# One product for q, k and v over two neighbouring PSUM banks, with the order of work rebuilt, in an attention and FFN block

## The chip, the cores and the metric

The kernel runs on one core of a Trainium2 chip. Five engines work side by side, each through its own queue in order: TensorE (PE in the profile, its weight loads PEld), VectorE (DVE), ScalarE (ACT), GpSimd (POOL) and SyncE (SP), which issues transfers. They wait for each other through semaphores. Times are microseconds of the device for one execution; lower is better.

## What is computed

For x of 8 batches x 512 rows x 128 columns:

```python
xn = _layernorm(x)                                  # over the 128 columns
# attention part
q, k, v = split(xn @ w_qkv.T)                       # 16 heads of 8
q = softmax(einsum('bhtd,hcd->bhtc', q, code) * scale) * scale
k = einsum('bhtd,hcd->bhtc', k, code) * scale
k_exp = exp(k - max(k, axis=2))                     # 2 codes a head, max over time
kv = cumsum(k_exp x v, axis=2) / (cumsum(k_exp, axis=2) + 1e-09)
attn = einsum('bhtc,bhtcd->bhtd', q, kv) @ w_out.T
# FFN part, every operand through a blockwise FP4 quantisation (blocks of 16)
h = silu(fp4(xn) @ fp4(w_gate).T) * (fp4(xn) @ fp4(w_up).T)
out = x + attn + fp4(h) @ fp4(w_down).T
```

## The kernel before

A batch of 512 rows is worked on as four tiles of 128 rows (`TILES`), all four side by side in one buffer of 512 columns. The code weights are folded into the q and k weights at the start, so that the product of a tile with `wqk_t` has only 64 columns: 32 for q (`HC`, the difference of the two codes of a head) and 32 for k. The product with `wv_t` has 128.

A batch runs through these stages. ScalarE normalises x into `xn`; TensorE transposes it into the PSUM bank `t_ps`, ScalarE copies it to `xn_t`. TensorE then makes v of the four tiles in `t_ps` (L1458) and, some time later, q and k of the four tiles in `a_ps` (L1591). ScalarE copies v out (`v_sb`, L556) and takes q out (`q_rel`, L674). VectorE reduces the maximum of k over the tiles (`k_max`, L1162), TensorE transposes it (L1692, in `t_ps`), VectorE reduces it to `k_negmax` (L1234), and TensorE adds it to k where k stands in `a_ps` (the shift, L1729). ScalarE writes the exponential of k into `kv` (L786). GpSimd multiplies v into it (L500) and adds up the four tiles (L337, L391, L436). TensorE makes the base of the cumulative sum over the 128 partitions in `a_ps` (L1450); VectorE adds it (L992), makes the denominators (`den`, L1002), which ScalarE inverts through a logarithm and an exponential (`den_log` L607, `a_ps` L609, called dexp below), and after `den_p` and `den_r` makes the normalised q, `q_n` (L1051). GpSimd multiplies it into `o_codes` (L375), TensorE transposes those into `t_ps` (L1660, L1661), ScalarE copies them to `o_t` (L714).

The FFN takes xn through the quantisation: `x_abs`, `x_max`, `x_recip` on VectorE, `x_r` on ScalarE, `yx` on GpSimd, a square on ScalarE into `s_ps`, then `sx` and `qx` on VectorE, `xq` on GpSimd, a transpose into `t_ps` (L1508) and the copy `xq_t` (L587). Four gate and four up products of 352 columns go through the banks `g_ps`, `u_ps0` and `u_ps1`; ScalarE applies silu, VectorE multiplies to `h`, and h is quantised the same way (`h_max`, `h_recip`, `h_r`, `yh`, square, `sh`, `qh`, `hq`), transposed through `h_ps` to `hq_t` and multiplied with the down weights into `o_ps`, where the attention output is added to it (L1410 to L1626). VectorE adds x (`out_sb`, L1187), SyncE stores.

silu and the logarithm and exponential stand in two table sets of ScalarE, so that each batch has two table loads (L629, L784).

The order is written out by hand, or rather as the result of a plan: each engine's block is a loop over steps, and each piece of work stands in it with its own offset (`b = step - 13`), so that one turn of the loop works on several batches at once. The last batch has its own pieces with fixed steps. Waits are written ahead of the piece that needs them; a wait that an earlier one covers is left out. There is one buffer of two for most data (`p = b % 2`) and one bank of PSUM for each of the names above. At the start, short products of constants into `o_ps` stand between TensorE's own work.

## Time and profile before

| | us |
|---|---|
| median of 3 runs | 145.97 |
| lowest, highest | 145.9, 146.12 |
| the profiled execution | 145.66 |
| its span, first to last instruction | 143.9 |

| engine | busy us | share of the span |
|---|---|---|
| PE | 135.2 | 94% |
| DVE | 126.0 | 88% |
| POOL | 120.9 | 84% |
| ACT | 115.2 | 80% |
| PEld | 112.8 | 78% |

The span is read as a head in which weights are prepared and the first batches come in, a middle in which each batch takes the same time (a period), and a tail in which the last batch drains. A busy share over the whole span mixes them, so stretches are looked at apart. Durations of neighbours on an engine overlap by about 0.1 us in the records; the time that an instruction costs its engine is from its start to the start of the next.

### The profile page before, as it was taken

How to read it: one execution, taken by the hardware profiler on the slowest of the kernel's cores; microseconds unless marked ns; L12 is line 12 of the kernel's file. 1: busy time of each engine (PE TensorE's matmuls, PEld its weight loads, DVE VectorE, ACT ScalarE, POOL GpSimd, SP SyncE). 2: the span in 40 equal slices, each digit the busy share in tenths (PEclk: the TensorE clock that was granted, in tenths of full speed). 3: DMA queues.
4: the chain of work that ended last, by engine and by line, in shares of the span. 5: the costliest groups of instructions: out<-in, count | busy, mean ns of one | idle time of the engine just before them, and what ended most of it. 6: DMA issues, size and time to landing. Idle time of an engine off the chain costs nothing.

```text
span 143.9 us, 2675 instructions
## 1 busy us (share of the span) xinstructions
PE 135.2 (94%) x909; PEld 112.8 (78%) x909; DVE 126.0 (88%) x340; ACT 115.2 (80%) x276; POOL 120.9 (84%) x130
## 2 busy tenths in 40 slices
PE   3979999999999999999999999999999998969793
PEld 3979987598869886988698869887988685839692
DVE  0899998999899899989998999899989995999841
ACT  0376788799999989998999899989995797597450
POOL 4567688579999999999889998999599999969920
DMA  4990000000000001000100010001000200010012
GB/s 115 344 343 9 2 0 2 0 0 7 0 0 0 0 5 73 0 0 2 73 5 0 2 73 0 5 0 73 0 0 0 77 0 0 27 48 5 0 73 73
DMA packets 4078, 5.16 MB, mean 36 GB/s; under 512 B 545, under 2 KB 2145, under 8 KB 4065
## 3 DMA queue, kind: packets, MB, share of 16 engines
q1 hardware_dynamic: 3088, 4.49, 8.9%
q10 hardware_dynamic: 976, 0.51, 1.2%
q8 instruction: 7, 0.11, 0.3%
q14 instruction: 7, 0.05, 0.1%
HBM read 2.90 MB, written 2.10 MB: 35 GB/s over the span
## 4 chain that ended last, share of the span: by engine, by line
PE 75%; DVE 11%; ACT 5%; POOL 3%; DMA 2%; issue 1%
PE t_ps L1458 5%; PE a_ps L1591 4%; PE a_ps L1450 3%; PE g_ps L1603 3%; PE u_ps L1570 3%; PE g_ps L1711 3%; PE t_ps L1757 3%; PE u_ps L1574 3%; PE g_ps L1571 3%; PE o_ps L1412 3%; PE u_ps L1654 2%; PE g_ps L1675 2%; PE u_ps L1685 2%; PE o_ps L1626 2%; PE o_ps L1540 2%; PE o_ps L1501 2%
## 5 line engine op out<-in xcount | busy, mean ns | idle before, releaser
L500 POOL TENSOR_TENSOR kv<-v_sb,kv 128x512 f32<-128x512 f32 x14 | 14.8, 1077 | 0.0
L375 POOL TENSOR_TENSOR o_codes<-kv,q_n 128x1024 f32<-128x1024 f32 x7 | 13.8, 1965 | 0.1
L461 POOL TENSOR_TENSOR hq<-qh,h_max 128x704 f32<-128x704 bf16 x7 | 9.7, 1383 | 3.4 <-DVE qh L1307 3.4
L696 ACT ACTIVATE xn<-x_all,shift,rstd 128x128 f32<-128x128 f32 x28 | 11.5, 481 | 0.0
L449 POOL TENSOR_TENSOR yh<-h,h_r 128x704 f32<-128x704 f32 x7 | 9.7, 1386 | 1.5 <-ACT h_r L727 1.5
L399 POOL TENSOR_TENSOR hq<-qh,h_max 128x704 f32<-128x704 bf16 x7 | 9.7, 1386 | 0.0
L516 POOL TENSOR_TENSOR yh<-h,h_r 128x704 f32<-128x704 f32 x7 | 9.7, 1384 | 0.0
L495 POOL TENSOR_TENSOR yx<-xn,x_r 128x512 f32<-128x512 f32 x7 | 7.4, 1058 | 2.6 <-ACT x_r L811 2.6
L992 DVE TENSOR_TENSOR kv<-kv,a_ps 128x1152 f32<-128x1152 f32 x7 | 9.4, 1344 | 0.0
L629 ACT ACT_TABLE_LOAD x7 | 9.0, 1283 | 0.1
L1591 PEld LDWEIGHTS a_ps<-wqk_t,xn_t 128*128 128x128 f32 x56 | 7.3, 191 | 1.3
L784 ACT ACT_TABLE_LOAD x6 | 7.7, 1283 | 0.1
L1458 PEld LDWEIGHTS t_ps<-wv_t,xn_t 128*128 128x128 f32 x56 | 6.9, 191 | 1.0 <-ACT xn_t L794 0.8
L430 POOL TENSOR_TENSOR xq<-qx,x_max 128x512 f32<-128x512 bf16 x7 | 7.4, 1058 | 0.2 <-DVE qx L1093 0.2
L1458 PE MATMUL t_ps<-wv_t,xn_t 128*128 128x128 f32 x56 | 7.6, 278 | 0.0
L1591 PE MATMUL a_ps<-wqk_t,xn_t 128*128 128x64 f32 x56 | 7.0, 268 | 0.0
L1660 PE MATMUL t_ps<-ident,o_codes 128*128 128x128 f32 x28 | 6.5, 273 | 0.0
L1661 PE MATMUL t_ps<-ident,o_codes 128*128 128x128 f32 x28 | 6.5, 272 | 0.0
L1192 DVE TENSOR_REDUCE h_max<-h 128x44 f32<-128x748 f32 x7 | 6.5, 922 | 0.0
L921 DVE TENSOR_REDUCE h_max<-h 128x44 f32<-128x748 f32 x7 | 6.2, 884 | 0.1
L1626 PE MATMUL o_ps<-wd_t,hq_t 128*128 128x128 f32 x42 | 5.8, 275 | 0.0
L1540 PE MATMUL o_ps<-wd_t,hq_t 128*128 128x128 f32 x42 | 5.8, 275 | 0.0
(404 smaller groups left out, 512.7 us busy)
## 6 DMA issues: line engine op xcount, KB each, us to landing
x_all<-x SPq DMA_DIRECT2D x8, 256.0 KB, 4.4
out<-out_sb SPq DMA_DIRECT2D x7, 256.0 KB, 2.0
...
```

The lines of the kernel that those rows point to most:

```text
L375: nc.gpsimd.tensor_tensor(o_codes[:, p, :, :].rearrange("p j (c w) -> p j c w", w=HEAD), kv[:, p, :, 0:KV].rearrange("p j (c w) -> p j c w ...
L399: nc.gpsimd.tensor_tensor(hq[:, 4 * p + 0:4 * p + 2, 0:FF].rearrange("p t (b k) -> p t b k", k=BLOCK), qh[:, p, 0 * FF:2 * FF].rearrange(" ...
L449: nc.gpsimd.tensor_tensor(blocks(yh[:, p, 0 * FF:2 * FF], PAIR * HB), h[:, p, 0 * HB:2 * HB, 0:BLOCK], spread(h_r[:, p, 0 * HB:2 * HB], PA ...
L461: nc.gpsimd.tensor_tensor(hq[:, 4 * p + 2:4 * p + 4, 0:FF].rearrange("p t (b k) -> p t b k", k=BLOCK), qh[:, p, 2 * FF:4 * FF].rearrange(" ...
L500: last = nc.gpsimd.tensor_tensor(heads(kv[:, p, :, c * D:(c + 1) * D]), heads(v_sb[:, p, :].rearrange("p (j d) -> p j d", j=TILES)), widen ...
L516: nc.gpsimd.tensor_tensor(blocks(yh[:, p, 2 * FF:4 * FF], PAIR * HB), h[:, p, 2 * HB:4 * HB, 0:BLOCK], spread(h_r[:, p, 2 * HB:4 * HB], PA ...
L629: nc.scalar.activation(silu[:, 1, :], g_ps[:, 0:FF], ACT.Silu).then_inc(silu1_done, 1)
L696: last = nc.scalar.activation(xn[:, p, j * D:(j + 1) * D], x_all[:, b, j * D:(j + 1) * D], ACT.Identity, bias=shift[:, b, j:j + 1], scale= ...
L992: nc.vector.tensor_tensor(kv[:, p, :, :], kv[:, p, :, :], a_ps[:, 0:ROW].unsqueeze(1).broadcast_to([P, TILES, ROW]), ALU.add).then_inc(bad ...
L1458: last = nc.tensor.matmul(t_ps[:, j * P:(j + 1) * P], xn_t[:, p, j * P:(j + 1) * P], wv_t[:, :], start=True, stop=True)
L1540: last = nc.tensor.matmul(o_ps[:, 2 * P:3 * P], hq_t[:, 2, c * P:(c + 1) * P], wd_t[:, c * P:(c + 1) * P], start=False, stop=(c == CHUNKS ...
L1591: last = nc.tensor.matmul(a_ps[:, 2 * j * HC:2 * (j + 1) * HC], xn_t[:, p, j * P:(j + 1) * P], wqk_t[:, :], start=(j == 0), stop=False, sk ...
```

## The change

A tile's q, k and v come from one product of 192 columns: the weights stand side by side in `wqkv_t`. The four tiles of a batch fill 384 columns each of two neighbouring banks, tiles 0 and 1 in the one that was `a_ps`, tiles 2 and 3 in the one that was `t_ps`; both are now halves of one tensor `at_ps`, and the other uses of the two names go on. The readers of q, k and v take both banks in one instruction. The transposed k maximum goes to the free columns 384 to 511 of the second bank. The shift is written as two products, one for each bank. The separate v product and its semaphore are gone. The order of all pieces on all engines was made anew for this (`DEPTH`, the number of steps of the loop, goes from 89 to 105), and a few pieces of the last batch are split differently.

```diff
-        wqk_t = sb("wqk_t", [P, 2 * HC])
-        wv_t = sb("wv_t", [P, D])
+        wqkv_t = sb("wqkv_t", [P, QKV])
...
-        t_ps = bank("t_ps")
-        a_ps = bank("a_ps")
+        at_ps = ctx.enter_context(nc.psum_tensor("at_ps", [P, 2, 512], f32))
+        a_ps, t_ps = at_ps[:, 0, :], at_ps[:, 1, :]
+        qkv_ps = at_ps[:, :, 0:2 * QKV].rearrange("p a (j c) -> p a j c", j=2)
...
-                        last = nc.tensor.matmul(t_ps[:, j * P:(j + 1) * P], xn_t[:, p, j * P:(j + 1) * P], wv_t[:, :], start=True, stop=True)
...
-                        last = nc.tensor.matmul(a_ps[:, 2 * j * HC:2 * (j + 1) * HC], xn_t[:, p, j * P:(j + 1) * P], wqk_t[:, :], start=(j == 0),
+                        last = nc.tensor.matmul(at_ps[:, j // 2, j % 2 * QKV:(j % 2 + 1) * QKV], xn_t[:, p, j * P:(j + 1) * P], wqkv_t[:, :], start=(j % 2 == 0),
...
-                    nc.tensor.matmul(a_ps[:, 0:2 * TILES * HC].rearrange("p (j c) -> p j c", j=TILES)[:, :, HC:], k_negmax[:, 0:1].broadcast_to([HC, P]),
+                    for a in range(2):
+                        last = nc.tensor.matmul(qkv_ps[:, a, :, HC:2 * HC], k_negmax[:, 0:1].broadcast_to([HC, P]),
...
+                    nc.scalar.activation(v_sb[:, p, :].rearrange("p (a j d) -> p a j d", a=2, j=2), qkv_ps[:, :, :, 2 * HC:], ACT.Copy).then_inc(vev_done, 1)
...
-                    nc.vector.tensor_reduce(k_max[:, :], a_ps[:, 0:2 * TILES * HC].rearrange("p (j c) -> p c j", j=TILES)[:, HC:, :], AX.X, ALU.max).then_inc(kmax_done, 1)
+                    nc.vector.tensor_reduce(k_max[:, :], qkv_ps[:, :, :, HC:2 * HC].rearrange("p a j c -> p c a j"), AX.XY, ALU.max).then_inc(kmax_done, 1)
...
-DEPTH = 89
-
+DEPTH = 105
```

The order on TensorE in the middle of the program, before, from the base product to the q/k product of the next batch but one (hq are the quantised h that are transposed, xq_t the quantised x):

```order
L1450 MATMUL a_ps<-kv,before 128x288 [waits add3_done,kexp_done]
L1458 MATMUL t_ps<-wv_t,xn_t 128x128 [waits xnt_done]
L1458 MATMUL t_ps<-wv_t,xn_t 128x128 x3
...
L1508 MATMUL t_ps<-ident,xq 128x128 [waits vev_done]
...
L1570 MATMUL u_ps<-wu_t,xq_t 128x352 [waits xqt_done]
L1571 MATMUL g_ps<-wg_t,xq_t 128x352
L1574 MATMUL u_ps<-wu_t,xq_t 128x352
L1591 MATMUL a_ps<-wqk_t,xn_t 128x64 [waits qn_done]
L1591 MATMUL a_ps<-wqk_t,xn_t 128x64 x3
L1603 MATMUL g_ps<-wg_t,xq_t 128x352 [waits silu1_done]
```

And after:

```order
L1371 MATMUL at_ps<-kv,before 128x288 [waits add3_done]
...
L1452 MATMUL at_ps<-ident,xq 128x128 [waits xq_done,xnt_done]
...
L1508 MATMUL g_ps<-wg_t,xq_t 128x352 [waits xqt_done]
L1526 MATMUL h_ps<-ident,hq 128x128 [waits hqt2_done]
L1526 MATMUL h_ps<-ident,hq 128x128 x2
L1547 MATMUL u_ps<-wu_t,xq_t 128x352
L1566 MATMUL at_ps<-wqkv_t,xn_t 128x192 [waits qn_done]
L1566 MATMUL at_ps<-wqkv_t,xn_t 128x192 x3
L1573 MATMUL g_ps<-wg_t,xq_t 128x352 [waits silu1_done]
```

The v product is gone from behind the base, xq's transposes wait for xq and xn_t and no longer for v's copy, and between the first gate product and q, k, v stand transposes of hq that wait for a copy of ScalarE.

The order on ScalarE around the second table load, before (L727 is h_r of the first pair of tiles, L786 the exponential of k):

```order
L718 ACTIVATE silu<-g_ps 128x352 [waits gate2_done]
L727 ACTIVATE h_r<-h_recip 128x44 [waits hrec0_done]
L732 ACTIVATE s_ps<-yh 128x352 [waits qh3_done]
L759 ACTIVATE hq_t<-h_ps 128x384 [waits hqT1_done]
L771 ACTIVATE silu<-g_ps 128x352 [waits gate3_done]
L784 ACT_TABLE_LOAD
L786 ACTIVATE kv<-a_ps 128x4x32 [waits kshift_done]
L794 ACTIVATE xn_t<-t_ps 128x512 [waits xnT_done]
```

And after (L733 is that h_r):

```order
L656 ACTIVATE silu<-g_ps 128x352 [waits gate2_done]
L667 ACTIVATE xn<-x_all,shift,rstd 128x128 x4
L689 ACTIVATE silu<-g_ps 128x352 [waits gate3_done]
L707 ACT_TABLE_LOAD
L711 ACTIVATE kv<-at_ps 128x4x32 [waits o_done,kshift_done]
L721 ACTIVATE s_ps<-yh 128x352 [waits qh3_done]
L733 ACTIVATE h_r<-h_recip 128x44
L765 ACTIVATE hq_t<-h_ps 128x384 [waits hqT1_done]
L782 ACTIVATE o_t<-at_ps 128x512 [waits oT_done]
```

h_r, a square and a copy moved from ahead of the table load to behind it.

The order on VectorE from the denominators to the first h and on to k_max, before (L1123 is the first h):

```order
L1002 SCALAR_TENSOR_TENSOR den<-kv,a_ps 128x4x16 [waits badd_done]
L1002 SCALAR_TENSOR_TENSOR den<-kv,a_ps 128x4x16
L1034 SCALAR_TENSOR_TENSOR sx<-s_ps,yx 128x512 [waits sqx_done]
L1038 TENSOR_TENSOR den_p<-a_ps,den 128x128 [waits dexp_done]
L1048 SCALAR_TENSOR_TENSOR den_r<-den_p,a_ps 128x128 [waits dprod_done]
L1051 SCALAR_TENSOR_TENSOR q_n<-a_ps,den_r 128x128 [waits denr_done]
L1093 SCALAR_TENSOR_TENSOR qx<-s_ps,sx 128x512
L1123 TENSOR_TENSOR h<-silu,u_ps 128x22x16 [waits up1_done,silu1_done]
...
L1162 TENSOR_REDUCE k_max<-a_ps 128x32 [waits qrel_done]
```

And after:

```order
L1318 SCALAR_TENSOR_TENSOR den<-kv,at_ps 128x4x16 [waits badd_done]
L1318 SCALAR_TENSOR_TENSOR den<-kv,at_ps 128x4x16
L1331 SCALAR_TENSOR_TENSOR sh<-s_ps,yh 128x352 [waits sqh0_done]
L1333 SCALAR_TENSOR_TENSOR qh<-s_ps,sh 128x352 [waits sh0_done]
L936 TENSOR_TENSOR den_p<-at_ps,den 128x128 [waits dexp_done]
L949 SCALAR_TENSOR_TENSOR den_r<-den_p,at_ps 128x128 [waits dprod_done]
L997 SCALAR_TENSOR_TENSOR q_n<-at_ps,den_r 128x128 [waits denr_done]
L1003 SCALAR_TENSOR_TENSOR sx<-s_ps,yx 128x512 [waits sqx_done]
L1054 SCALAR_TENSOR_TENSOR qx<-s_ps,sx 128x512 [waits sx_done]
L1060 TENSOR_TENSOR h<-silu,u_ps 128x22x16 [waits up1_done,silu1_done]
...
L1102 TENSOR_REDUCE k_max<-at_ps 128x32 [waits vev_done]
```

sh and qh stand between den and den_p where sx stood, sx and qx stand together behind q_n, and k_max waits for v's copy.

## Rows read from the trace of the kernel before

**Rows 1.** Windows: stretch, length, PE PEld DVE ACT POOL busy, clock, DMA share, GB/s.

```profile
58.10:72.60 14.50, 14.50 (x100) 11.96 (x99) 13.66 (x32) 13.41 (x32) 13.71 (x13) 1.00 0.05 19
```

**Rows 2.** Chain of work that ended last, in order of time: start, length, what.

```profile
58.58 0.68 PE a_ps L1450 x2
...
73.09 0.67 PE a_ps L1450 x2
```

**Rows 3.** Timeline of TensorE: start, length, line, out<-in, count; one period.

```profile
59.09 1.06 PE L1458 MATMUL t_ps<-wv_t,xn_t 128*128 128x128 f32 x8
59.99 0.49 PE L1491 MATMUL h_ps<-ident,hq 128*128 128x128 f32 x3
...
64.05 0.76 PE L1574 MATMUL u_ps<-wu_t,xq_t 128*128 128x352 f32 x2
64.65 1.00 PE L1591 MATMUL a_ps<-wqk_t,xn_t 128*128 128x64 f32 x8
65.48 0.81 PE L1603 MATMUL g_ps<-wg_t,xq_t 128*128 128x352 f32 x2
...
70.80 0.48 PE L1729 MATMUL a_ps<-ident,k_negmax 32*128 32x128 f32 x2
71.21 0.66 PE L1757 MATMUL t_ps<-ident,xn 128*128 128x128 f32 x4
```

**Rows 4.** Timeline of VectorE in the same period; in brackets idle time and its releaser.

```profile
62.04 0.35 DVE L1002 SCALAR_TENSOR_TENSOR den<-kv,a_ps 128x64 f32<-128x64 f32 x2
62.31 0.68 DVE L1034 SCALAR_TENSOR_TENSOR sx<-s_ps,yx 128x512 f32<-128x512 f32 x1
63.37 0.29 DVE L1038 TENSOR_TENSOR den_p<-a_ps,den 128x128 f32<-128x128 f32 x1 [0.38 <-ACT a_ps L609]
...
64.22 0.68 DVE L1093 SCALAR_TENSOR_TENSOR qx<-s_ps,sx 128x512 bf16<-128x512 f32 x1
65.14 0.52 DVE L1123 TENSOR_TENSOR h<-silu,u_ps 128x352 f32<-128x352 f32 x1 [0.24 <-ACT silu L629]
65.58 0.52 DVE L1128 SCALAR_TENSOR_TENSOR sh<-s_ps,yh 128x352 f32<-128x352 f32 x1
66.13 0.52 DVE L1154 SCALAR_TENSOR_TENSOR qh<-s_ps,sh 128x352 bf16<-128x352 f32 x1
66.58 0.28 DVE L1162 TENSOR_REDUCE k_max<-a_ps 128x32 f32<-128x128 f32 x1
```

**Rows 5.** Timeline of ScalarE in the same period.

```profile
61.85 0.60 ACT L587 ACTIVATE xq_t<-t_ps 128x512 f32<-128x512 f32 x1
62.34 0.48 ACT L600 ACTIVATE hq_t<-h_ps 128x384 f32<-128x384 f32 x1
62.71 0.31 ACT L607 ACTIVATE den_log<-den 128x128 f32<-128x128 f32 x1
63.05 0.28 ACT L609 ACTIVATE a_ps<-den_log 128x128 f32<-128x128 f32 x1
63.35 1.28 ACT L629 ACT_TABLE_LOAD   x1
64.65 0.46 ACT L629 ACTIVATE silu<-g_ps 128x352 f32<-128x352 f32 x1
...
69.64 0.23 ACT L727 ACTIVATE h_r<-h_recip 128x44 f32<-128x44 f32 x1
```

**Rows 6.** Timeline of GpSimd in the same period.

```profile
72.36 1.38 POOL L461 TENSOR_TENSOR hq<-qh,h_max 128x704 f32<-128x704 bf16 x1 [0.79 <-DVE qh L1307]
```

**Rows 7.** Timeline of VectorE: the first q_n and the sixth.

```profile
35.31 0.29 DVE L1051 SCALAR_TENSOR_TENSOR q_n<-a_ps,den_r 128x128 f32<-128x128 f32 x1
...
107.53 0.29 DVE L1051 SCALAR_TENSOR_TENSOR q_n<-a_ps,den_r 128x128 f32<-128x128 f32 x1
```

**Rows 8.** Timeline of ScalarE in the head: the variance steps' first, the table load.

```profile
21.11 0.20 ACT L603 ACTIVATE var_eps<-meanvar 128x8 f32<-128x8 f32 x1
...
22.05 1.28 ACT L629 ACT_TABLE_LOAD   x1
```

More of the change, by code:

```diff
@@ L997, in _ @@
[L997 to L1005 removed]
+                    dve.wait_ge(sqx_done, b + 1)
@@ L1167, in _ @@
+                if step == 5:
+                    for j in range(TILES):
+                        last = nc.vector.bn_aggr(meanvar[:, 1, j, :], stats[:, 1, j, :])
+                    last.then_inc(aggr_done, 1)
                 if step == 15:
@@ L1174, in _ @@
                     p = b % 2
[L1175 to L1180 removed]
+                    dve.wait_ge(silu3_done, b + 1)
@@ new lines, in _ @@
+                if step == 70:
+                    b = BATCHES - 1
+                    p = b % 2
+                    pe.wait_ge(hqt2_done, 8)
+                    nc.tensor.matmul(t_ps[:, 2 * P:3 * P], o_t[:, p, 2 * P:3 * P], wo_t[:, :], start=True, stop=False)
+                    for c in range(CHUNKS):
+                        last = nc.tensor.matmul(t_ps[:, 2 * P:3 * P], hq_t[:, 2, c * P:(c + 1) * P], wd_t[:, c * P:(c + 1) * P], start=False, stop=(c == CHUNKS - 1))
+                    last.then_inc(down2_done, 1)
@@ new lines, in _ @@
+                if step == 30:
+                    b = BATCHES - 1
+                    p = b % 2
+                    pe.wait_ge(ot_done, 6)
+                    pe.wait_ge(xq_done, 8)
+                    for j in range(TILES):
+                        last = nc.tensor.transpose(t_ps[:, j * P:(j + 1) * P], xq[:, p, j * P:(j + 1) * P], ident[:, :])
+                    last.then_inc(xqT_done, 1)
+                if step == 22:
+                    for _ in range(2):
+                        nc.tensor.matmul(o_ps[:, 0:P], ident[:, :], before[:, :], start=True, stop=True)
@@ new lines, in _ @@
+                if step == 23:
+                    for _ in range(2):
+                        nc.tensor.matmul(o_ps[:, 0:P], ident[:, :], before[:, :], start=True, stop=True)
+                if step == 29:
+                    b = BATCHES - 1
+                    p = b % 2
+                    pe.wait_ge(ot_done, 5)
+                    for j in range(TILES):
+                        last = nc.tensor.transpose(t_ps[:, j * P:(j + 1) * P], xn[:, p, j * D:(j + 1) * D], ident[:, :])
+                    last.then_inc(xnT_done, 1)
@@ new lines, in _ @@
+                b = step - 23
+                if 0 <= b < BATCHES - 1:
+                    p = b % 2
+                    pe.wait_ge(xnt_done, b + 2)
+                    pe.wait_ge(xq_done, b + 1)
+                    for j in range(TILES):
+                        last = nc.tensor.transpose(t_ps[:, j * P:(j + 1) * P], xq[:, p, j * P:(j + 1) * P], ident[:, :])
+                    last.then_inc(xqT_done, 1)
+                if step == 24:
+                    for _ in range(2):
+                        nc.tensor.matmul(o_ps[:, 0:P], ident[:, :], before[:, :], start=True, stop=True)
@@ new lines, in _ @@
+                if step == 23:
+                    pe.wait_ge(wev_done, 1)
+                    for c in range(CHUNKS):
+                        last = nc.tensor.transpose(h_ps[:, c * P:(c + 1) * P], w_dq[:, FFP + c * P:FFP + (c + 1) * P], ident[:, :])
+                    last.then_inc(wT_done, 1)
+                if step == 30:
+                    b = BATCHES - 1
+                    p = b % 2
+                    nc.tensor.matmul(u_ps[0][:, 0:FF], xq_t[:, p, 0 * P:1 * P], wu_t[:, :], start=True, stop=True).then_inc(up0_done, 1)
@@ new lines, in _ @@
+                b = step - 25
+                if 0 <= b < BATCHES - 1:
+                    p = b % 2
+                    nc.tensor.matmul(o_ps[:, 0 * P:1 * P], o_t[:, p, 0 * P:1 * P], wo_t[:, :], start=True, stop=False)
+                    for c in range(CHUNKS):
+                        last = nc.tensor.matmul(o_ps[:, 0 * P:1 * P], hq_t[:, 0, c * P:(c + 1) * P], wd_t[:, c * P:(c + 1) * P], start=False, stop=(c == CHUNKS - 1))
+                    last.then_inc(down0_done, 1)
+                b = step - 23
@@ new lines, in _ @@
+                if step == 46:
+                    b = BATCHES - 1
+                    p = b % 2
+                    pe.wait_ge(hqz1_done, 1)
+                    for c in range(CHUNKS):
+                        last = nc.tensor.transpose(g_ps[:, c * P:(c + 1) * P], hq[:, 4 * p + 1, c * P:(c + 1) * P], ident[:, :])
+                    last.then_inc(hqT1_done, 1)
+                if step == 7:
+                    for _ in range(2):
+                        nc.tensor.matmul(o_ps[:, 0:P], ident[:, :], before[:, :], start=True, stop=True)
@@ L1357, in _ @@
+                if step == 4:
+                    for _ in range(2):
+                        nc.tensor.matmul(o_ps[:, 0:P], ident[:, :], before[:, :], start=True, stop=True)
+                if step == 59:
                     b = BATCHES - 1
@@ L1379, in _ @@
[L1379 to L1387 removed]
+                    pe.wait_ge(add3_done, 8)
```

2202 lines of the change are left out of this document (1067 added, 1135 removed).

## The prediction

> **What bounds the kernel now.** I read the table of windows first, then the chain of work that ended last, then the timelines of the four engines over one period, and last the ends of the run. The windows show TensorE busy for all of 14.5 us in a middle stretch, with VectorE and GpSimd at 13.7 and ScalarE at 13.4, at a granted clock of 1.00 [rows 1]: four engines are nearly full, so the reader should expect a gain on one to meet the next at once. In the chain the same product (the base of the cumulative sum) comes back 14.51 us later [rows 2]. That is the period of one batch.
>
> TensorE's own work in a period is less than 14.51. From start to start, 128 columns cost 0.111 us per pass (the v product, 8 passes, 59.09 to 59.99 with the hop: 0.90), 352 columns 0.295 (two passes in 0.59), and the q/k product of 64 columns 0.84 for 8 passes, so 0.105 each: it is paced by its weights and not by its columns [rows 3]. Summed over the order that stands ahead (v 0.89, q/k 0.84, eight 352-column products 4.74, output products 3.56, transposes 2.86, base 0.50, shift 0.22, and the rest 0.31) this is 13.9; some 0.6 is waiting, mostly around the shift (0.41 from its start to the next, for 0.22 of work) and around the v product [rows 3].
>
> VectorE: 14.51 less what its waits cost. Its wait for den_p stretches sx from 0.60 to 1.06 (62.31 to 63.37), that for the first h stretches qx from 0.60 to 0.92 (64.22 to 65.14), and a third, not shown, costs 0.08: own work 13.65 [rows 4]. GpSimd waits 0.79 for qh each period [rows 6]; own work 13.66.
>
> **The change part by part.**
>
> 1. *The product.* Removed: v 0.89 and q/k 0.84 = 1.73. Added: 8 passes of 192 columns. Between 128 columns (0.111) and 352 (0.295) a column costs 0.00082, so a pass costs 0.111 + 64 x 0.00082 = 0.164, eight 1.31. Bounds: 1.28 by the 352-column pace per column alone, 1.73 if nothing is saved by the join. Gain 0.42.
>
> 2. *The shift.* One product of 128 columns becomes two of 64. Its 2 passes become 4; the nearest row is the 64-column pass, 0.105, so 0.42 in place of 0.22: a loss of 0.20, bounds 0 and 0.27. TensorE's own work becomes about 13.9 - 0.42 + 0.20 = 13.7. So the arithmetic of the join is worth only 0.2 us a period, and 13.7 is also what VectorE and GpSimd need. The order decides.
>
> 3. *Reads over two banks* (q_rel, v_sb, k_max, exp of k). No row has such a read. Nearest are the same counts from one bank: 0.28 for 128 elements, 0.60 for 512 [rows 4, 5]. I take no change; bounds 0 and +50%, since below nothing there is no reason for a gain and a second start could cost at most a piece of the 0.2 us that a small read is.
>
> 4. *The new order, one period.* I walk it from the start of q_n = 0, with durations from start to start.
> VectorE, from the first den: den 0.27, sh and qh 0.94 (the pair from 65.58 took 1.00), den_p, den_r and q_n 0.85 (63.37 to 64.22), sx 0.71, qx 0.60 = 3.37 until the first h. ScalarE over the same stretch: den ready 0.35, hop 0.06, den_log 0.33, dexp 0.30, hq_t 0.37, the square for sx 0.60 (the table load starts only when it has ended), table load 1.30, silu 0.46, hop 0.04 = 3.81 [rows 4, 5]. So the first h waits 0.44. The wait for dexp is gone (sh and qh cover it, where before only sx did), but qh now stands directly behind its sh and qx behind its sx: a dependent pair costs 0.55 where an independent one costs 0.44 (h, sh, qh from 65.14 [rows 4]), two pairs 0.2.
> TensorE: hq_t ends at -0.3, its transposes run to 0.17, up1 to 0.76, q/k/v 0.76 to 2.09, gate0 and up0 to 3.27, end 3.43; the second h starts at 3.47 and could have at 3.41. v_sb ends at 3.83, k_max can start at 3.91. k_max's transpose 4.66 to 4.93, k_negmax wants it at 5.00. Shift 6.84 to 7.4. ScalarE's second table load ends at 7.97, exp of k at 8.27; the transposes of o start at 8.48, o_t ends 10.14, xn transposed 10.9, xn_t 11.53, xq transposed 12.30, xq_t 12.93, gate1 13.36, and the next q/k/v could start at 15.02: TensorE alone would close in 14.26.
> VectorE closes at: own work 13.65 + 0.2 for the pairs + 0.44 + 0.06 = **14.34**.
> GpSimd: h_r of the first pair stood right behind a silu and ahead of the table load (69.64); it now stands behind the load, the exp and a square, at 8.5 instead of 5.6 after q_n [rows 5]. The yh that waits for it moves to 8.7, the hq after it then waits for qh until 10.7, 0.62. 13.66 + 0.62 + 0.07 of hops = 14.35. GpSimd runs 2.5 us later against VectorE than it did, which its readers bear: hq done 6.9, wanted 8.15; yh 10.1, wanted 11.55; hq 12.07, wanted 12.14.
> Period 14.34 against 14.51: -0.17. From the first q_n to the sixth are five periods (the first is shorter in both, as no output sum stands in it yet): -0.9.
>
> 5. *The head.* Before, the first q_n starts at 35.31 [rows 7]. On ScalarE the first silu table load starts at 22.05, behind five small steps of the variance that start at 21.11, after xq_t [rows 8]. In the new order x is normalised ahead of the weights' factors, since the memsets and the w_r step no longer stand ahead of it, and the variance steps stand ahead of xq_t, where ScalarE waited anyway. My walk gives xn(0) from 6.7, q/k/v(0) at 12.25, exp of k at 16.9 (no gain so far), but xq_t at 19.3 and the table load at 20.8: -1.2. Then h of batch 0 at 22.8, second table load 27.3, base 29.0, q_n 33.4: -1.9. What is late next there is the yx square (20.2), which waits for GpSimd. Bounds: 0 (all given back at a wait that I missed) and -2.3.
>
> 6. *The tail.* From the sixth q_n (107.53 [rows 7]) to the end are 36.4 us. Same walk: the seventh q_n 13.80 later (13.69 before); the last base 20.07 (19.44), the last sum 21.9, last q_n 25.45 (24.82), o codes 27.75 (27.13); then yh stands directly behind the codes and o_t no longer waits for it, so the last output products run from 29.64 and end at 34.0 (33.9). +0.1; bounds -0.5 and +0.8.
>
> Sum: span 143.9 - 0.9 - 1.9 + 0.1 = 141.2. The profiled execution took 145.66, 1.76 more than its span, so 142.96; the median of the runs is 0.31 above it: **143.3 us**.
>
> **A rule weighed.** What the order shows: k_max waited only for q_rel, which reads the same bank; now it waits for v_sb, which ends 1.0 us later in my walk (3.83), as q, k and v share the banks. It costs nothing while h stands ahead of it on VectorE, and the margin is 0.08. The Trainium skill, PSUM — Partial Sum Buffer, section "PSUM bank collisions raise a hardware error", says that no two engines may access one bank in one quadrant at once, two readers included, and tells to guard by bank. By that rule every reader of the pair stands in a queue. No run here shows a collision; the waits in the order are what that rule asks for. It names no price; what a late queue costs is the slow rival below, whose numbers come from the rows.
>
> **Rivals.**
> - *Only the head gains* (period stays 14.5, as a margin of 0.06 to 0.08 is missed somewhere, or all four queues drift): 145.97 - 1.9 + 0.1 = 144.2. For it: four engines at 93% or more [rows 1], and k_negmax and hq fit by 0.07. Against: TensorE has 0.08 and gate1 0.4 to spare.
> - *No change*: the join saves nothing and the head's gain is taken back at base: 145.7 to 146.2. For it: TensorE is not the bound of the new period anyway.
> - *Slower: the two banks become one chain.* q/k/v, q_rel, v_sb, k_max, its transpose, k_negmax, shift, table load, exp, o transposes, o_t, xn, xn_t, xq, xq_t, and then q/k/v again; before, the v product had this bank apart from q and k. Its slack in my walk is 0.2 at o and 0.4 at gate1. It decides from the point where k_max starts more than 0.08 late: k_negmax then misses its place, and if the four reads take half as long again (0.14 + 0.30 + 0.14 + 0.14 = 0.7) the period is 14.34 + 0.7 - 0.1 = 14.9 to 15.0. Six such periods: +2.7, less 1.9 + 0.1: 146.9. Against it: a read's time follows its elements in every row, 0.28 for 128 and 0.60 for 512 [rows 4, 5].
> - *Better*: GpSimd's wait of 0.62 and the h wait overlap less than I add, period 14.1, and the tail gives 0.5: 141.6.
>
> **How the numbers follow.** Forecast 0.51 (142.3 to 144.0), head only 0.20, better 0.08, no change 0.07, slower 0.14. A measurement of this kernel tells about 0.2% (0.3 us) from no change. Faster by more than that: 0.51 + 0.20 + 0.08 = 0.79; same 0.07; slower 0.14. The range must leave out no more than 0.2: half of the better case and most of the slow one lie outside 141.9 to 145.8, which also takes in 0 for the head's gain together with the shorter period.
>
> **What would show it.** Right: q/k/v passes 0.16 apart and the shift four passes 0.105 apart; base to base 14.3 to 14.4; VectorE's waits in a period only at the first h (about 0.4) and hardly at den_p; GpSimd waiting at hq for qh 0.6 and its o codes 2.5 us behind q_n; the first silu table load near 20.8 and the first q_n near 33.4; from the sixth q_n to the end 36 to 37. Wrong: q_rel or v_sb over 0.35 or 0.7; k_max waiting for v_sb, k_negmax for TensorE; a period over 14.5; a first q_n after 34.5.

## Result, and the profile of the changed kernel

The changed kernel takes 145.08 us (median of 22 runs, 144.70 to 146.65), the kernel before 145.96 us (median of 22 runs beside it, 145.57 to 146.19). The ratio is 0.9955, with a 95% interval of 0.9937 to 0.9972: faster by 0.45%, 0.9 us, where 2.7 us was forecast. The time lies within the range that was given.

The profiled execution took 144.95 us, its span is 142.9 us. The windows show the same stretch as [rows 1]: TensorE still without a pause, VectorE and GpSimd a little fuller than before.

```profile
58.10:72.60 14.50, 14.50 (x93) 11.69 (x92) 13.84 (x32) 13.29 (x32) 13.83 (x13) 1.00 0.05 19
```

The timeline of VectorE gives the first, second and sixth q_n, in place of [rows 7]:

```profile
34.16 0.29 DVE L997 SCALAR_TENSOR_TENSOR q_n<-at_ps,den_r 128x128 f32<-128x128 f32 x1
48.04 0.29 DVE L997 SCALAR_TENSOR_TENSOR q_n<-at_ps,den_r 128x128 f32<-128x128 f32 x1
...
105.99 0.29 DVE L997 SCALAR_TENSOR_TENSOR q_n<-at_ps,den_r 128x128 f32<-128x128 f32 x1
```

With these the span falls into the three stretches of the forecast. The last column is run e1 below, the changed kernel with one operand of its shift widened.

| stretch, us | before | forecast | after | e1 |
|---|---|---|---|---|
| to the first q_n | 35.31 | 33.4 (-1.9) | 34.16 (-1.15) | 34.48 (-0.83) |
| first to sixth q_n | 72.22 | 71.3 (-0.9) | 71.83 (-0.39) | 70.60 (-1.62) |
| sixth q_n to the end | 36.37 | 36.5 (+0.1) | 36.91 (+0.54) | 36.52 (+0.15) |
| span | 143.9 | 141.2 | 142.9 | 141.6 |

All three stretches gave less than forecast. Of the 0.39 in the middle, 0.31 are the first period alone (13.88 for 14.19); the four behind it take 14.48 to 14.50, where they took 14.50 to 14.51. The period of a batch, which was to fall by 0.17, has hardly moved. e1's head is the longer one by a transfer that landed late and not by its edit, as the experiments on the head show.

In the head, ScalarE's timeline has xn, the first exponential of k, and the table load, in place of [rows 8]:

```profile
6.58 1.65 ACT L667 ACTIVATE xn<-x_all,shift,rstd 128x128 f32<-128x128 f32 x4 [1.31 <-POOL shift L531]
...
17.42 0.28 ACT L711 ACTIVATE kv<-at_ps 128x128 f32<-128x128 f32 x1 [0.35 <-PE at_ps L1684]
...
21.30 1.28 ACT L579 ACT_TABLE_LOAD   x1
```

The load is 0.75 earlier than before (22.05), not 1.2. The period in the middle is 14.48, by two base products on TensorE's timeline (which stand where [rows 2] has its base):

```profile
57.85 0.65 PE L1371 MATMUL at_ps<-kv,before 128*128 128x288 f32 x2
...
63.28 1.46 PE L1566 MATMUL at_ps<-wqkv_t,xn_t 128*128 128x192 f32 x8
64.58 0.84 PE L1573 MATMUL g_ps<-wg_t,xq_t 128*128 128x352 f32 x2
65.27 0.75 PE L1574 MATMUL u_ps<-wu_t,xq_t 128*128 128x352 f32 x2
65.98 0.86 PE L1584 MATMUL g_ps<-wg_t,xq_t 128*128 128x352 f32 x2
66.68 0.76 PE L1592 MATMUL u_ps<-wu_t,xq_t 128*128 128x352 f32 x2
...
68.79 0.83 PE L1668 MATMUL o_ps<-wd_t,hq_t 128*128 128x128 f32 x6
69.55 0.65 PE L1684 MATMUL at_ps<-ident,k_negmax 32*128 32x64 f32 x4
70.13 0.49 PE L1726 MATMUL o_ps<-wo_t,o_t 128*128 128x128 f32 x2
70.46 0.83 PE L1728 MATMUL o_ps<-wd_t,hq_t 128*128 128x128 f32 x6
...
72.33 0.65 PE L1371 MATMUL at_ps<-kv,before 128*128 128x288 f32 x2
```

Read the starts. The joined product takes 63.28 to 64.58, 1.30 for its eight passes: the 0.164 a pass of the forecast. The gate products (L1573, L1584) take 0.69 and 0.70 to the next start, not 0.59: each starts on a silu that ends at the last moment. And the shift (L1684) takes far more than its four passes of 0.105. Six passes of the output product from 68.79 end at 69.46 (0.67, as everywhere); the shift starts at 69.55, the next product at 70.13, and that one, L1726, takes 0.33 where it takes 0.22 elsewhere. From 69.46 to 70.24 are 0.78 us. The kernel before has the same gaps, by two rows of its TensorE timeline that stand around those of [rows 3]:

```profile
70.11 0.76 PE L1711 MATMUL g_ps<-wg_t,xq_t 128*128 128x352 f32 x2
...
71.71 0.49 PE L1354 MATMUL h_ps<-ident,hq 128*128 128x128 f32 x3
```

The gate product is over at 70.70 (0.59), the shift starts at 70.80, and the four transposes behind it take 0.50 (71.21 to 71.71) where they take 0.44 elsewhere: 70.70 to 71.27, 0.57 us for two passes.

On VectorE the wait for the first h is as the forecast said. The profile has 0.36 of idle time; from start to start, the measure of the forecast, qx takes 1.05 where it takes 0.60 without a wait, so 0.45 (0.44 forecast). At den_p the forecast had 0.06, and it is 0.18: qh to den_p takes 0.62, and 0.44 in e1, where the result of dexp is early enough:

```profile
60.43 0.35 DVE L1318 SCALAR_TENSOR_TENSOR den<-kv,at_ps 128x64 f32<-128x64 f32 x2
60.70 0.52 DVE L1331 SCALAR_TENSOR_TENSOR sh<-s_ps,yh 128x352 f32<-128x352 f32 x1
61.26 0.52 DVE L1333 SCALAR_TENSOR_TENSOR qh<-s_ps,sh 128x352 bf16<-128x352 f32 x1
61.88 0.29 DVE L936 TENSOR_TENSOR den_p<-at_ps,den 128x128 f32<-128x128 f32 x1
...
63.50 0.69 DVE L1054 SCALAR_TENSOR_TENSOR qx<-s_ps,sx 128x512 bf16<-128x512 f32 x1
64.55 0.52 DVE L1060 TENSOR_TENSOR h<-silu,u_ps 128x352 f32<-128x352 f32 x1 [0.36 <-ACT silu L579]
```

GpSimd waits twice in a period (0.36 for h_r, 0.31 for qh) instead of once [rows 6], 0.67 in all; the forecast had 0.62, all of it at qh:

```profile
58.68 1.38 POOL L351 TENSOR_TENSOR hq<-qh,h_max 128x704 f32<-128x704 bf16 x1 [0.31 <-DVE qh L1289]
...
71.41 1.39 POOL L346 TENSOR_TENSOR yh<-h,h_r 128x704 f32<-128x704 f32 x1 [0.36 <-ACT h_r L733]
```

### The profile page after: what moved, and what is told of

Same layout as the page of the kernel before. It is cut to its first block, busy times and chain, and to the rows that moved or that the text cites. A ratio compares the mean times of both kernels' runs of the same rounds, so it can differ in the third digit from the quotient of the medians.

```text
span 142.9 us, 2597 instructions
## 1 busy us (share of the span) xinstructions
PE 135.8 (95%) x861; PEld 111.0 (78%) x861; DVE 126.4 (88%) x340; ACT 114.3 (80%) x276; POOL 120.9 (85%) x130
## 4 chain that ended last, share of the span: by engine, by line
PE 72%; ACT 8%; DVE 7%; POOL 6%; DMA 3%; issue 2%; SPq 1%; ACTq 0%
PE at_ps L1566 6%; PE g_ps L1584 3%; DMA w_raw<-w_up 3%; PE g_ps L1573 3%; PE o_ps L1502 3%; PE o_ps L1444 3%; PE g_ps L1508 3%; PE u_ps L1642 2%; PE u_ps L1547 2%; PE g_ps L1644 2%; PE u_ps L1592 2%; PE u_ps L1574 2%; PE at_ps L1684 2%; PE at_ps L1371 2%; PE o_ps L1728 2%; PE o_ps L1668 2%
## 5 line engine op out<-in xcount | busy, mean ns | idle before, releaser
L1566 PEld LDWEIGHTS at_ps<-wqkv_t,xn_t 128*128 128x128 f32 x56 | 9.3, 190 | 2.2 <-DVE q_n L997 0.8
L1566 PE MATMUL at_ps<-wqkv_t,xn_t 128*128 128x192 f32 x56 | 10.5, 330 | 0.4 <-DVE q_n L997 0.3
L1307 DVE TENSOR_TENSOR kv<-kv,at_ps 128x1152 f32<-128x1152 f32 x7 | 9.4, 1337 | 0.0
L1766 PE MATMUL at_ps<-ident,o_codes 128*128 128x128 f32 x28 | 6.5, 274 | 0.1
L1767 PE MATMUL at_ps<-ident,o_codes 128*128 128x128 f32 x28 | 6.5, 273 | 0.0
L1573 PE MATMUL g_ps<-wg_t,xq_t 128*128 128x352 f32 x14 | 6.0, 507 | 0.1
L1584 PE MATMUL g_ps<-wg_t,xq_t 128*128 128x352 f32 x14 | 6.0, 511 | 0.0
L782 ACT ACTIVATE o_t<-at_ps 128x512 f32<-128x512 f32 x7 | 4.2, 595 | 2.1 <-PE at_ps L1767 2.1
L1728 PE MATMUL o_ps<-wd_t,hq_t 128*128 128x128 f32 x42 | 5.8, 275 | 0.0
```

The lines of the kernel that those rows point to most:

```text
L1307: nc.vector.tensor_tensor(kv[:, p, :, :], kv[:, p, :, :], a_ps[:, 0:ROW].unsqueeze(1).broadcast_to([P, TILES, ROW]), ALU.add).then_inc(bad ...
L1566: last = nc.tensor.matmul(at_ps[:, j // 2, j % 2 * QKV:(j % 2 + 1) * QKV], xn_t[:, p, j * P:(j + 1) * P], wqkv_t[:, :], start=(j % 2 == 0) ...
L1573: nc.tensor.matmul(g_ps[:, 0:FF], xq_t[:, p, 0 * P:1 * P], wg_t[:, :], start=True, stop=True).then_inc(gate0_done, 1)
L1584: nc.tensor.matmul(g_ps[:, 0:FF], xq_t[:, p, 2 * P:3 * P], wg_t[:, :], start=True, stop=True).then_inc(gate2_done, 1)
```

## Experiments

Two theories stood against each other first. **A**: TensorE is the bound of the new period, and what was mis-sized is the shift, since products whose weights have 32 rows cost it more than their passes. **B**: the gaps around the shift belong to its waits, and another engine closes the period.

**e1, weights of 128 rows.** `k_negmax` gets 128 rows, zero from row 32 on, and meets all rows of the identity's first 32 columns. The result and the columns are the same.

```diff
-        k_negmax = sb("k_negmax", [HC, 1])
+        k_negmax = sb("k_negmax", [P, 1])
...
-                        last = nc.tensor.matmul(qkv_ps[:, a, :, HC:2 * HC], k_negmax[:, 0:1].broadcast_to([HC, P]),
-                                                ident[0:HC, 0:HC].unsqueeze(1).broadcast_to([HC, 2, HC]), start=False, stop=True, skip_group_check=True)
+                        last = nc.tensor.matmul(qkv_ps[:, a, :, HC:2 * HC], k_negmax[:, 0:1].broadcast_to([P, P]),
+                                                ident[:, 0:HC].unsqueeze(1).broadcast_to([P, 2, HC]), start=False, stop=True, skip_group_check=True)
```

> The changed kernel, with the shift's weights (k_negmax) widened from 32 rows to 128 by zeros; same result, same columns. Theory A (TensorE is the bound of the new period, and products with weights of 32 rows cost it more than their passes: in the changed kernel 69.46 to 70.24, so 0.78 us, for four passes of 0.105): the passes then lie 0.105 apart, the shift costs 0.42 to 0.45, the period falls from 14.48 by 0.15 (if VectorE or GpSimd, at 14.3, stop it) to 0.36, six times, so the whole by 0.9 to 2.2 us, to 143.0 to 144.2. Theory B (the gaps around the shift come from its late start, k_negmax, or ScalarE's chain sets the period): the same time within 0.2 us, and still 0.1 ahead of the shift and 0.1 behind it.

Measured: 143.25 us, ratio to the kernel before 0.981 (0.978 to 0.984), so 1.8 us less than the changed kernel. TensorE's timeline, one period:

```profile
57.84 0.65 PE L1372 MATMUL at_ps<-kv,before 128*128 128x288 f32 x2
...
68.78 0.83 PE L1669 MATMUL o_ps<-wd_t,hq_t 128*128 128x128 f32 x6
69.45 0.56 PE L1685 MATMUL at_ps<-ident,k_negmax 128*128 128x64 f32 x4
69.85 0.44 PE L1727 MATMUL o_ps<-wo_t,o_t 128*128 128x128 f32 x2
70.12 0.83 PE L1729 MATMUL o_ps<-wd_t,hq_t 128*128 128x128 f32 x6
...
71.99 0.65 PE L1372 MATMUL at_ps<-kv,before 128*128 128x288 f32 x2
```

Up to 68.78 all starts of the period are those of the changed kernel to 0.01 us. The shift then follows at once (69.45) and takes 0.40, what stands behind it comes 0.34 earlier, and the period is 14.15: it falls by the 0.33 that TensorE saves. The weight loads, on the timeline of TensorE's loads, show what changes. First the changed kernel, then e1:

```profile
69.55 0.52 PEld L1684 LDWEIGHTS at_ps<-ident,k_negmax 32*128 32x128 f32 x4
70.13 0.30 PEld L1726 LDWEIGHTS o_ps<-wo_t,o_t 128*128 128x128 f32 x2
```

```profile
69.34 0.53 PEld L1685 LDWEIGHTS at_ps<-ident,k_negmax 128*128 128x128 f32 x4
69.79 0.30 PEld L1727 LDWEIGHTS o_ps<-wo_t,o_t 128*128 128x128 f32 x2
```

With 32 rows the first load starts together with its product, 69.55, though k_negmax has been ready since 67.9 (on VectorE it runs from 67.58 for 0.28); with 128 rows it starts 0.11 ahead of its product, 69.34, under the product before. The load behind the shift starts with its product too in the one (70.13) and 0.06 ahead in the other. The wait for k_negmax stands in both programs at the same place, so theory B falls, and theory A holds for both of its halves. The edit widens both operands of the product, the weights and what streams past them; which of the two makes the cost no run separates.

**e2, e3: the same questions in the old order.** e2 widens the one shift product of the kernel before, in the same way; e3 cuts it in two and leaves its 32 rows:

```diff
-                    nc.tensor.matmul(a_ps[:, 0:2 * TILES * HC].rearrange("p (j c) -> p j c", j=TILES)[:, :, HC:], k_negmax[:, 0:1].broadcast_to([HC, P]),
+                    for a in range(2):
+                        last = nc.tensor.matmul(a_ps[:, 0:2 * TILES * HC].rearrange("p (j c) -> p j c", j=TILES)[:, 2 * a:2 * a + 2, HC:], k_negmax[:, 0:1].broadcast_to([HC, P]),
```

> The kernel before with the same widening of its one shift product of 128 columns. Theory A: there the shift costs 0.57 (70.70 to 71.27) for two passes of 0.11; widened about 0.25; if TensorE sets that period too, it falls from 14.51 by up to 0.3 and the whole by up to 1.8 us, to 144.2; if VectorE's waits for dexp set it, by less than 0.3 us. Theory B: the same time within 0.2 us.

> The kernel before with its one shift product of 128 columns cut into two of 64, still 32 rows of weights: the cost of the cut alone in the old order. Theory A: the shift takes 0.58 from start to next instead of 0.41, 0.17 to 0.2 more per period, and the time grows by up to 1.2 us (147.1) if TensorE sets the old period, by nothing if VectorE does. Theory B (the cut costs nothing, gaps belong to the wait): 145.9 to 146.2.

Measured: e2 145.52 us, ratio 0.9976 (0.9959 to 0.9993); e3 146.18, ratio 1.003 (1.0007 to 1.0053). The shift costs what theory A says: in e2 0.22, from 71.57 to 71.79, with no gap on either side; in e3 0.59 instead of 0.41 to the next start (71.06 to 71.65). But the period is 14.50 in e2 and 14.51 in e3, that of the kernel before. In e2 TensorE's saving comes back at the base, five groups of products behind the shift, as a wait for the exponential of k on ScalarE:

```profile
71.57 0.38 PE L1730 MATMUL a_ps<-ident,k_negmax 128*128 128x128 f32 x2
71.79 0.60 PE L1758 MATMUL t_ps<-ident,xn 128*128 128x128 f32 x4
...
73.87 0.75 PE L1451 MATMUL a_ps<-kv,before 128*128 128x288 f32 x2 [0.27 <-ACT kv L786]
```

So TensorE was busy all the time in the old order and did not bound it: 0.35 us taken off it there bought nothing in the period, and 0.18 put on it cost nothing. The kernel before shows the wait already, though its rows give it no idle time (timeline of TensorE, then of ScalarE):

```profile
57.75 0.83 PE L1412 MATMUL o_ps<-wd_t,hq_t 128*128 128x128 f32 x6
58.51 0.75 PE L1450 MATMUL a_ps<-kv,before 128*128 128x288 f32 x2
```

```profile
58.18 0.28 ACT L786 ACTIVATE kv<-a_ps 128x128 f32<-128x128 f32 x1
```

The output product is over at 58.42 (0.67), the exponential ends at 58.46, the base starts at 58.51 and takes 0.58 to the next start. In e3, where the shift brings TensorE there later, the base starts at once and takes 0.51. The 0.09 ahead of the base and the 0.07 in it are what swallowed the 0.18. What closes the old period is thus a path through ScalarE's second table load and that exponential; which engine it passes on the way was not tested. Outside the period e3 is 0.25 us slower: from the first q, k product to the first q_n it takes 22.53, where the kernel before takes 22.20 and e2 22.09. The profiled execution of e2 is the slowest of its twelve (146.53; VectorE waits 0.96 for the transfer of w_up), so the stretches of its trace account for 0.2 of its gain of 0.4 us (0.11 in the head, 0.09 up to the sixth q_n), and the rest stays open.

**e4, the join undone in place.** The changed kernel, with two products for a tile again, into the same columns of the same banks:

```diff
-                        last = nc.tensor.matmul(at_ps[:, j // 2, j % 2 * QKV:(j % 2 + 1) * QKV], xn_t[:, p, j * P:(j + 1) * P], wqkv_t[:, :], start=(j % 2 == 0),
+                        nc.tensor.matmul(at_ps[:, j // 2, j % 2 * QKV:j % 2 * QKV + 2 * HC], xn_t[:, p, j * P:(j + 1) * P], wqkv_t[:, 0:2 * HC], start=(j % 2 == 0),
+                                         stop=False, skip_group_check=True)
+                        last = nc.tensor.matmul(at_ps[:, j // 2, j % 2 * QKV + 2 * HC:(j % 2 + 1) * QKV], xn_t[:, p, j * P:(j + 1) * P], wqkv_t[:, 2 * HC:], start=False,
```

> The changed kernel with the join undone in its place: for each row group one product of 64 columns (q, k) and one of 128 (v) into the same places of the same banks, in the new order. Theory A (TensorE bounds the new period): the product costs 1.73 instead of 1.30, the period is 14.9, and the time 6 to 8 times 0.43 more: 147.7 to 148.3. Theory B (another engine bounds it): 0 to 1 us more, 145.1 to 146.1.

Measured: 148.12 us, ratio 1.015 (1.0126 to 1.0174), period 14.88. The products take 65.04 to 66.83, 1.79 instead of 1.30; the gate product behind them gives 0.1 back, as its silu is done by then. The period grows by 0.40. In the new order a microsecond of TensorE is a microsecond of the period, and the join is worth 3.0 us of the whole. The new order without the join is 2.2 us slower than the kernel before.

**e5, h_r back ahead of the table load.** On ScalarE the block of L733 stands ahead of the load and the exponential of k again (with its wait for h_recip in every batch).

> The changed kernel with the first pair's h_r put back ahead of the second table load on ScalarE, so that GpSimd need not wait for it (0.36 us a period there). Theory A (TensorE alone bounds the new period): GpSimd's wait for h_r goes and comes back at its next wait, the period stays at 14.48, the time within 0.3 us of 145.1. Theory B (the forecast's walk, where GpSimd with this wait closes its own loop at 14.35 and so is among the bounds): up to 0.3 us a period less, 143.3 to 144.5.

Measured: 145.62 us, ratio 0.9971 (0.995 to 0.9991), an interval that overlaps that of the changed kernel. The period is 14.48 still. GpSimd no longer waits for h_r, and waits 0.61 for qh instead of 0.31. That wait was free.

**e6 to e8, the gate products.** On top of e1: the first up product of a batch ahead of its gate product, the fourth up product ahead of the third gate product, v's copy and k_max ahead of the silu and the h that they stood behind. TensorE's part:

```diff
+                    nc.tensor.matmul(u_ps[0][:, 0:FF], xq_t[:, p, 0 * P:1 * P], wu_t[:, :], start=True, stop=True).then_inc(up0_done, 1)
                     pe.wait_ge(silu1_done, b + 1)
                     nc.tensor.matmul(g_ps[:, 0:FF], xq_t[:, p, 0 * P:1 * P], wg_t[:, :], start=True, stop=True).then_inc(gate0_done, 1)
-                    nc.tensor.matmul(u_ps[0][:, 0:FF], xq_t[:, p, 0 * P:1 * P], wu_t[:, :], start=True, stop=True).then_inc(up0_done, 1)
```

> The kernel with the widened shift, and on TensorE the first up product of a batch put ahead of its gate product and the fourth up product ahead of the third gate product (on ScalarE the copy of v then stands ahead of that silu, on VectorE k_max ahead of that h), so that no gate product stands right behind the end of the silu that it waits for. Theory A (each product that starts on a wait costs TensorE 0.1 us over its 0.59, three of them in a period): the gate products lie 0.59 apart, the period falls from 14.15 by 0.2 to 0.3, to 13.85 to 13.95, if VectorE (own work 13.8) allows it; the time is 141.5 to 142.5. Theory B (those 0.1 us belong to the products, or VectorE's wait of 0.34 for its first h is now what closes the period): 143.0 to 143.6; or slower, to 144.5, if the later gate products hold up ScalarE.

> The same as the last one with TensorE's order alone changed, ScalarE and VectorE left as they were. It tells what the silu, which now ends some 0.35 us later, costs where its followers are not moved out of its way: ScalarE waits 0.35 for the first gate product with the copy of v queued behind it. Theory A: half of the gain, 142.3 to 143.2. Theory B: no gain or slower, 143.2 to 144.5.

> e6 with h_r ahead of the second table load too. Once TensorE's gaps are gone, VectorE and GpSimd stand at their own work (13.7 to 13.8), so GpSimd's wait for h_r should begin to count. Theory A: 0.1 a period less than e6, 0.2 to 0.8 us in all. Theory B (GpSimd still has room, or the exp of k, now 0.12 later, costs as much): the time of e6 within 0.3 us.

Measured: 146.16, 145.89 and 146.26 us, all 2.6 to 3.0 more than e1; period 14.6 in e6 and e7. I had this wrong by some 4 us. The first gate product does take 0.59 now (the third still 0.69), but VectorE gets a second wait, since the silu of the first gate comes later (timeline of VectorE in e6):

```profile
66.06 0.52 DVE L1061 TENSOR_TENSOR h<-silu,u_ps 128x352 f32<-128x352 f32 x1 [0.34 <-ACT silu L579]
...
68.01 0.52 DVE L1094 TENSOR_TENSOR h<-silu,u_ps 128x352 f32<-128x352 f32 x1 [0.23 <-ACT silu L629]
```

In e1 VectorE's only pause in a period of 14.15 is the 0.34 at its first h, and that one cannot be filled, as e9 shows; it has no room for another wait. So e1 already stands at two bounds at once, and a wait moved from TensorE to VectorE lengthened the period by 0.5. e8's earlier h_r changed nothing (0.1 from e6).

**e9, transposes of the fourth hq moved.** On top of e1: these three transposes go from ahead of the second up product to ahead of the third gate product, and the copy of the third hq_t from ahead of the first silu's table load to behind that silu.

> The kernel with the widened shift (e1), and the transposes of the fourth hq moved on TensorE from ahead of the second tile's up product to ahead of the third gate product; on ScalarE the copy of the third hq_t stands behind the first silu and its square instead of ahead of the silu's table load, and the copy of the fourth behind the square that follows v. Theory A (TensorE's gaps of 0.1 at products that start on a wait are the bound, and a gap goes where the wait is met earlier): the table load and the first silu come 0.37 earlier, the first gate product no longer waits for it, the third gate product has 0.33 of transposes between it and the first silu that it waits for; three gaps, 0.3, go, the period is 13.85 to 13.95 (VectorE's own work is 13.8), and the time 141.2 to 142.2. Theory B (as in e6, the move makes a new wait on VectorE or ScalarE): 143.2 or more.

Measured: 144.08 us, ratio 0.9889 (0.9842 to 0.9937), 0.8 more than e1; period 14.34. The copy is gone from ahead of the table load, but the load does not move, because the square between them waits for VectorE's qh (timeline of ScalarE):

```profile
61.03 0.28 ACT L880 ACTIVATE at_ps<-den_log 128x128 f32<-128x128 f32 x1
61.69 0.60 ACT L571 ACTIVATE s_ps<-yx 128x512 f32<-128x512 bf16 x1 [0.39 <-DVE qh L1334]
62.31 1.28 ACT L575 ACT_TABLE_LOAD   x1
```

qh reads `s_ps`, which the square overwrites. So qh, this square, the load, the silu and the first h are one chain, and VectorE's wait of 0.34 belongs to it. I had read the busy ScalarE as the cause, and it only covered that wait. The 0.19 by which the period grew are small late starts on VectorE, the largest of them k_negmax, 0.09.

**e10, e11, the head.** e10 is e1 with two moves ahead of the first period: VectorE's w_s of w_down behind the first k_negmax, and TensorE's first transposes of the weights behind the first shift. e11 is e9 with them.

> e1 with two moves in the head only: on VectorE one step of the weights (w_s of w_down) stands behind the first k_negmax instead of ahead of it, and on TensorE the first transposes of the weights stand behind the first shift. It tests what kept the head's gain at 1.1 us where 1.9 was forecast. Theory A (the chain through the two banks, k_max to exp of k at 17.42 instead of 16.9, is what is late there): exp of k of batch 0 at 16.6 to 16.8, the first silu table load at 20.5 instead of 21.3, the first q_n at 33.4 to 33.8, and 0.5 to 0.9 us less than e1. Theory B (GpSimd's yx and its followers bound the head): the table load at 21.1 to 21.4, the time within 0.3 us of e1.

> e9 and e10 together. Theory A: the gains add, as they lie in different stretches: 140.5 to 141.6. Theory B: the better of the two within 0.3 us.

Measured: e10 142.84 us, ratio 0.9793 (0.9762 to 0.9823); e11 143.86, ratio 0.985 (0.9823 to 0.9877). The intervals overlap those of e1 (0.978 to 0.984) and e9 (0.9842 to 0.9937), so a gain of the two moves is not shown. In e10 the exponential of k runs at 17.24 and the table load at 21.05, not 20.5: ScalarE holds the exponential back behind two variance steps that wait 0.63 for VectorE. The first q_n is at 33.76, 0.72 ahead of e1's, but this is not the work of the moves. The heads have to be compared behind the same event. In every trace of the new order the first product of q, k and v starts 4.22 to 4.24 us behind VectorE's reduction of w_down, and when that starts hangs on transfers:

| | reduction of w_down | first q, k, v | first q_n | q, k, v to q_n |
|---|---|---|---|---|
| after | 8.29 | 12.52 | 34.16 | 21.64 |
| e1 | 9.02 | 13.24 | 34.48 | 21.24 |
| e9 | 8.65 | 12.88 | 34.12 | 21.24 |
| e10 | 8.13 | 12.35 | 33.76 | 21.41 |
| e11 | 8.47 | 12.70 | 34.10 | 21.40 |
| e12 | 8.30 | 12.53 | 35.13 | 22.60 |
| e13 | 8.24 | 12.48 | 34.62 | 22.14 |

In e1's profiled execution VectorE waits 0.90 for x of the second batch:

```profile
8.07 0.87 DVE L1110 BATCH_NORM_STATS2 stats<-x_all 128x6 f32<-128x128 f32 x4 [0.90 <-DMA x_all<-x]
```

Behind q, k, v the two moves of e10 and e11 lose 0.17, and the widened shift of e1 gains 0.40.

**e12, e13, the second batch's statistics.** On VectorE they move behind the first batch's x_recip; e12 is the changed kernel with this, e13 is e10 with it.

```diff
-                if step == 5:
-                    dve.wait_ge(x_in[1], 16)
-                    for j in range(TILES):
-                        last = nc.vector.bn_stats(stats[:, 1, j, :], x_all[:, 1, j * D:(j + 1) * D])
-                    last.then_inc(stats_done, 1)
```

> The changed kernel with one move in the head: on VectorE the statistics of the second batch (0.79, and the 0.3 that sum them up) stand behind the first batch's x_abs, x_max and x_recip instead of ahead of them. Theory A (the head's gain of 1.9 was forecast from xn, which does end 1.6 us earlier, but VectorE takes x_abs up only 0.9 after xn's end, behind these statistics and the weights' steps): x_abs at 8.4 instead of 9.1, q/k/v of batch 0 at 11.7 to 11.9 instead of 12.5, the first q_n 0.5 to 0.8 earlier, and the time 144.3 to 144.7. Theory B (the chain through k_max and the shift, or GpSimd's w_y, is what is late): the first q_n at 34.0 to 34.3, the time within 0.2 us of 145.1.

> e10 (widened shift, the two moves in the head) with the same move of the statistics. Theory A: 0.5 to 0.8 us less than e10, 142.0 to 142.4. Theory B: the time of e10 within 0.2 us.

Measured: e12 145.12 us, ratio 0.995 (0.9934 to 0.9967), so no change; e13 143.51, ratio 0.9852 (0.9815 to 0.9889), 0.7 more than e10. Theory A was wrong. VectorE's timeline of the changed kernel, then of e12:

```profile
6.46 0.95 DVE L1021 TENSOR_REDUCE w_abs<-w_raw 128x48 f32<-128x768 f32 x1 [0.46 <-DMA w_raw<-w_up]
7.35 0.87 DVE L1109 BATCH_NORM_STATS2 stats<-x_all 128x6 f32<-128x128 f32 x4
8.14 0.23 DVE L1117 TENSOR_REDUCE w_max<-w_abs 128x48 f32<-128x96 f32 x1
8.29 0.51 DVE L1169 TENSOR_REDUCE w_abs<-w_raw 128x22 f32<-128x352 f32 x1
...
9.13 0.67 DVE L1199 TENSOR_REDUCE x_abs<-xn 128x32 f32<-128x512 f32 x1
```

```profile
7.18 0.25 DVE L1113 TENSOR_REDUCE w_max<-w_abs 128x48 f32<-128x96 f32 x1
8.30 0.52 DVE L1165 TENSOR_REDUCE w_abs<-w_raw 128x22 f32<-128x352 f32 x1 [0.86 <-DMA w_raw<-w_down]
...
9.15 0.67 DVE L1195 TENSOR_REDUCE x_abs<-xn 128x32 f32<-128x512 f32 x1
```

x_abs starts at 9.15 with the statistics gone: behind them stood a wait of 0.86 for the transfer of w_down, which they had filled. In these executions the weights' transfers set x_abs, and the statistics now push back what stands behind them (w_s of the gate at 13.07, before it 12.01). Behind q, k, v that costs e12 0.96 and e13 0.73, and the 0.73 is what e13 loses. e12's profiled execution took 146.05, where five others lie at 144.94 to 145.26; that w_down landed earlier in those and gave the loss back would fit, but no trace shows it. That x_abs placed ahead of both reductions would be earlier was not tried.

## Why the prediction was wrong in size and right in sign

**The step that failed: part 2, the shift, and with it the TensorE line of the walk.** The forecast priced the shift by its passes, 0.22 before and 0.42 after, and took the rest of its 0.41 us for waiting, which a better order would remove. It is no waiting: k_negmax is ready 1.6 us ahead in the changed kernel and 0.5 in the one before (70.26 for 70.80). It is a cost of a product with 32 rows, 0.33 to 0.35 us a period in either kernel (e1, e2), and in the new order, where TensorE bounds the period, all of it counts. The difference of the two shifts, 0.21, was right (0.20 forecast), yet the walk charged 0.42 where 0.78 is due (it writes "Shift 6.84 to 7.4", but its 8.48 for the transposes of o leaves 7.26 for the end of the shift, with 1.22 for the products between). The rows of before showed it, 0.57 for two passes, had it been measured to the first normal start. The Trainium skill, TensorE: Matmul & The Clock Gate, section "LDWEIGHTS (loading the stationary operand)", says that a weight load of 32 rows takes as long as one of 128. The load's own time agrees here (0.18 and 0.19); what a product of 32 rows among products of 128 costs is more than that, as e1 shows.

**A second, smaller miss: starts on a wait.** Against the walk (relative to q_n at 62.52) the third gate product is on time, 3.46 for 3.48 (the 4.66 of k_max's transpose less two products of 0.59); k_max's transpose is 0.09 late, as this gate product takes 0.70. The shift starts at 7.03 for 6.84, the third output product at 7.61 for 7.26, the transposes of o at 8.93 for 8.48. Of this 0.45, 0.1 is the gate's and 0.35 the shift's. The walk then goes on as foretold, o_t, xn, xq through the one bank, and den_log starts 0.80 behind den (60.43 to 61.23) where it had 0.41. TensorE closes at 14.48 and not at 14.26, and so TensorE, not VectorE, is the bound of the new period (e1 and e4).

**VectorE's 14.34 was too long.** e1 runs at 14.15 with all of its work: from start to start the wait for the first h costs 0.43 (0.44 forecast), den_p nothing (0.06 forecast), and own work is 13.72 (13.85 forecast). With the shift repaired the period is shorter than forecast. The 14.35 for GpSimd was no bound either: e1 passes it, and in e5 its wait was free.

**The product, the reads, the pairs: right.** 1.30 for 1.31; q_rel and v_sb 0.28 and 0.59; the period's gain from the join 0.40 (e4) for 0.42.

**The rule weighed, and the slow rival.** k_max's wait for v_sb cost nothing, as forecast; no run here shows a collision. The one chain through the two banks exists (shift, o transposes, o_t, xn_t, xq_t, next q, k, v). Its slack was used up by the shift and not by reads over two banks, so the rival's price was wrong. Whether this chain or TensorE's queue, through which its products pass without a pause, closes at 14.48 no run separates. The rival "only the head gains" (144.2, a period of 14.5) comes nearest to what was measured.

**The head: -1.15 for -1.9.** xn starts at 6.58 (6.7 forecast). q, k, v start at 12.52 (12.25), the exponential of k is at 17.42 (16.9), the table load at 21.30 (20.8), q_n at 34.16 (33.4). Of the 0.76, 0.27 are lost ahead of q, k, v, on VectorE, which waits 0.46 for the transfer of w_up, a wait that the forecast does not name. The other 0.49 lie behind: 21.64 to the first q_n for 21.15 forecast. e1 takes 21.24 there, so 0.40 of them are the shift's again. How the 0.27 could be had stays open; e12 and e13 moved the wrong piece.

**The tail: +0.54 for +0.1.** Its first step is one more period, 14.27 for 13.80. In e1 it is 13.87 and the tail +0.15. So the tail's miss is the shift's again.

**The right total, by luck in part.** With the shift alone repaired, e1 takes 143.25 us where 143.3 was forecast. Two misses meet in this: its middle is 0.7 shorter than forecast (70.60 for 71.3), and the head of its profiled execution 1.1 longer (34.48 for 33.4).
